# Second layer norm in place in the residual tile, eight normalises and two additions on VectorE, and last batches of three and one

## The reference

```python
# attention: favor-style, 16 heads of 16
q, k = favor(x @ Wq + bq), favor(x @ Wk + bk)   # favor: softmax over the 16 features of a head
probs = (q @ k.T) / (sum(q) + EPS)
x = layernorm(x + (probs @ (x @ Wv + bv)) @ Wo + bo)
# FFN with blockwise FP4 quantise-dequantise of every operand (blocks of 16), inner width 704
gate, up = fp4(x) @ fp4(w_gate).T, fp4(x) @ fp4(w_up).T
x = layernorm(x + fp4(silu(gate) * up) @ fp4(w_down).T)
```

## Time and profile before

| | |
|---|---|
| three runs, us | 706.77, 708.69, 709.64 (median 708.69) |
| profiled execution, us | 707.44, of which span 705.70 |
| busy share of the span | TensorE 97%, its weight loads 93%, VectorE 89%, ScalarE 82%, GpSimd 80% |
| granted TensorE clock, mean | 0.995 |
| 64 stores | 128 KB each, 1.7 us from issue to landing |

### The profile page before, as it was taken

The page is one execution under the profiler, slowest core; times in us unless marked ns, Lnnn a source line. Parts: engine busy times, 40 slices in busy tenths (PEclk is TensorE's granted clock), DMA queues, the critical chain, the costliest instruction groups (busy, mean ns, idle before and its releaser), DMA issues.

```text
span 705.7 us, 16440 instructions
## 1 busy us (share of the span) xinstructions
PE 681.2 (97%) x4782; PEld 656.9 (93%) x4782; DVE 627.4 (89%) x1498; ACT 577.1 (82%) x1355; POOL 562.0 (80%) x581
## 2 busy tenths in 40 slices
PE   6999999999999979999999999999999999999993
PEld 5999999999998869999999999999999999999983
DVE  3999988999998989999999989989899998999874
ACT  5888888887778978898877777778777898888887
POOL 3778778788877878888888898888888888888760
PEclk9999999999999999999999999999999999999999
DMA  5323322223222100000000000000000011011114
GB/s 164 94 73 86 87 76 78 83 68 91 83 79 80 39 16 1 1 2 1 1 1 2 1 2 1 2 1 1 1 1 2 25 37 47 31 46 46 51 62 142
DMA packets 40473, 30.16 MB, mean 43 GB/s; under 512 B 3776, under 2 KB 40384, under 8 KB 40384
## 3 DMA queue, kind: packets, MB, share of 16 engines
q1 hardware_dynamic: 37648, 26.88, 12.7%
q10 hardware_dynamic: 2736, 2.23, 1.1%
HBM read 20.71 MB, written 8.39 MB: 41 GB/s over the span
## 4 chain that ended last, share of the span: by engine, by line
PE 88%; ACT 4%; DVE 3%; issue 3%; DMA 1%; POOL 1%; ACTq 0%; SPq 0%; DVEq 0%; POOLq 0%
PE bank L820 66%; PE wide L938 6%; PE wide L820 5%; PE bank L853 4%; PE bank L931 2%; PE bank L851 2%; PE wide L882 2%; PE bank L921 1%; PE bank L919 1%; DMA bias_b<-L_attn_bk 1%; ACT scratch L480 1%; PE wide L865 0%; ACT dump L475 0%; ACT res L480 0%; ACT bank L449 0%
## 5 line engine op out<-in xcount | busy, mean ns | idle before, releaser
L820 PE MATMUL bank<-wf_hi,rounded 128*128 128x352 f32 (+1 forms) x1664 | 387.0, 310 | 4.0 <-DVE res L768 1.7
L820 PEld LDWEIGHTS bank<-wf_hi,rounded 128*128 128x128 f32 x1664 | 283.9, 189 | 5.2 <-issue 3.9
L820 PE MATMUL bank<-wf_lo,rounded 128*128 128x352 f32 (+1 forms) x832 | 255.2, 307 | 0.0
L820 PEld LDWEIGHTS bank<-wf_lo,rounded 128*128 128x128 f32 x832 | 157.6, 189 | 0.0
L820 PE MATMUL bank<-qkv_hi,rounded 128*128 128x512 f32 (+1 forms) x512 | 146.4, 349 | 3.1 <-ACT bank L449 3.1
L416 POOL TENSOR_TENSOR scratch<-scratch 128x704 f32<-128x704 bf16 x64 | 94.9, 1482 | 38.9 <-DVE scratch L794 38.9
L820 PEld LDWEIGHTS bank<-qkv_hi,rounded 128*128 128x128 f32 x512 | 93.0, 191 | 14.2 <-issue 3.6
L405 POOL TENSOR_TENSOR scratch<-scratch 128x704 bf16<-128x704 f32 x64 | 98.3, 1536 | 1.9 <-ACT scratch L596 1.9
L376 POOL TENSOR_TENSOR scratch<-scratch 128x512 f32<-128x512 f32 x64 | 68.0, 1063 | 39.0 <-DVE scratch L707 38.8
L411 POOL TENSOR_TENSOR scratch<-scratch 128x704 f32<-128x704 f32 x64 | 89.3, 1395 | 3.7 <-DVE scratch L765 3.7
L820 PE MATMUL bank<-qkv_lo,rounded 128*128 128x512 f32 (+1 forms) x256 | 87.1, 340 | 0.0
(11 more groups left out here) (98 smaller groups left out, 1563.7 us busy)
## 6 DMA issues: line engine op xcount, KB each, us to landing
scratch<-x_feat SPq DMA_DIRECT2D x64, 128.0 KB, 2.2
scratch<-x_tok SPq DMA_DIRECT2D x64, 128.0 KB, 2.4
out<-scratch SPq DMA_DIRECT2D x64, 128.0 KB, 1.7
scratch<-w_ffn ACTq DMA_DIRECT2D x15, 128.0 KB, 2.3
scratch<-L_attn_Wq SPq DMA_DIRECT2D x1, 256.0 KB, 3.2
scratch<-L_attn_Wk SPq DMA_DIRECT2D x1, 256.0 KB, 3.4
scratch<-L_attn_Wv SPq DMA_DIRECT2D x1, 256.0 KB, 6.0
wo<-L_attn_Wo SPq DMA_DIRECT2D x1, 256.0 KB, 4.5
```

What stands on the lines that cost most here:

```text
L820: op = pe.matmul(dst, x(c), w(c), start=first and n == 0, stop=last and n == len(terms) - 1, skip_group_check=not first)
```

## The change

The normalises of the second norm write into the residual tile itself, the four buffers `o_t` and the wait for their stores go, and the stores read from `res`. The odd tiles from 49 to 63 are normalised by VectorE (a tensor_scalar at the end of its step), the others by ScalarE as before. The batches of the second norm start at other steps: those of 8 and of 4 tiles one step earlier, and the last four tiles are a batch of three (from step 68) and a batch of one (from step 70). The addition h_c of tiles 62 and 63 moves from GpSimd to VectorE, just ahead of h_g and behind slot 0 of the next step. One more round of steps is added at the end so that all of it has its place.

```diff
--- before.py
+++ after.py
@@ -48,7 +48,9 @@
 LN_SLOTS = {1: (4,), 2: (1, 5), 3: (0, 3, 6), 4: (0, 2, 4, 6), 7: (0, 1, 2, 3, 4, 5, 6)}
 LN_A = ((0, 32, 1, 44), (32, 32, 2, 82))
 SQUARE_AT = tuple(range(9, 41)) + tuple(61 + k * 2 // 3 for k in range(32))
-LN_B = ((0, 32, 2, 38), (32, 16, 2, 54), (48, 8, 4, 62), (56, 4, 7, 66), (60, 4, 7, 70))
+LN_B = ((0, 32, 2, 38), (32, 16, 2, 54), (48, 8, 4, 61), (56, 4, 7, 65), (60, 3, 7, 68), (63, 1, 7, 70))
+LAST = 62
+BY_DVE = (49, 51, 53, 55, 57, 59, 61, 63)
 
 
 def need(eng, sem, count):
@@ -183,9 +185,6 @@
         bmx, binv = ([part(NB) for _ in range(2)] for _ in range(2))
         bs2 = [part(11 * (NB // 11 + 1)).rearrange("p (a b) -> p a b", a=11)[:, :, 0:NB // 11] for _ in range(2)]
         assert taken[0] <= until_post
-        taken[0] = until_post
-        o_t = [part(D) for _ in range(T)]
-        assert taken[0] <= until_x_in
         taken[0] = until_x_in
         hg = [part(I // 2, BF16) for _ in range(2)]
         assert taken[0] <= until_x_bo
@@ -215,18 +214,18 @@
         e_max, e_s2s, e_invs, e_xns, e_ys, e_mgs, e_cs, e_gs, x_q = (
             sem(f"e_{k}") for k in "max s2 inv xn y mg c g q".split())
         x_t, x_hi, x_lo = sem("x_t"), sem("x_hi"), sem("x_lo")
-        gu_a, gu_b, si_a, si_b, h_a, h_b, h_max, h_s2, h_inv, h_xn, h_y, h_mg, h_c, h_g, h_q = (
+        gu_a, gu_b, si_a, si_b, h_a, h_b, h_max, h_s2, h_inv, h_xn, h_y, h_mg, h_c, h_cd, h_g, h_q = (
             sem(f"b_{k}") for k in
-            "gua gub sia sib ha hb hmax hs2 hinv hxn hy hmg hc hg hq".split())
-        h_t, h_hi, h_lo, h_dup, d_s, y_s, y_sq, y_ln, y_o = (
-            sem(f"b_{k}") for k in "ht hhi hlo hdup d y ysq yln yo".split())
+            "gua gub sia sib ha hb hmax hs2 hinv hxn hy hmg hc hcd hg hq".split())
+        h_t, h_hi, h_lo, h_dup, d_s, y_s, y_sq, y_ln, y_o, y_od = (
+            sem(f"b_{k}") for k in "ht hhi hlo hdup d y ysq yln yo yod".split())
 
         block = ctx.enter_context(nc.Block())
 
 
 
         A_FROM, A_TO = -1, NS + 16
-        B_FROM, B_TO = -2, NS + 3
+        B_FROM, B_TO = -2, NS + 4
         JOIN = NT + 3
 
         def ready(m, batches):
@@ -323,8 +322,12 @@
             def stores(i):
                 for t in range(T):
                     m = T * i + t
-                    sp.wait_ge(y_o, m + 1)
-                    sp.dma_start(out[bass.ds(m * P, P), :], o_t[t]).then_inc(st_out[t], 16)
+                    by_dve = sum(n <= m for n in BY_DVE)
+                    if m in BY_DVE:
+                        sp.wait_ge(y_od, by_dve)
+                    else:
+                        sp.wait_ge(y_o, m + 1 - by_dve)
+                    sp.dma_start(out[bass.ds(m * P, P), :], res[:, rows(m)]).then_inc(st_out[t], 16)
 
             for i in range(0, NS):
                 stores(i)
@@ -399,10 +402,11 @@
                     pool.tensor_tensor(blocks(xq[:, n % T * D:(n % T + 1) * D]), blocks(e_g[e][:, half]),
                                        over(e_s2[p % 3][:, scales], XB), ALU.mult).then_inc(x_q, 1)
                 for n in tile(m - 2):
-                    need(pool, h_xn, n + 1)
-                    need(pool, h_g, n - 1)
-                    need(pool, h_mg, n + 1)
-                    pool.tensor_tensor(hc[n % 2], hxn[n % 2], hmg[n % 2], ALU.add).then_inc(h_c, 1)
+                    if n < LAST:
+                        need(pool, h_xn, n + 1)
+                        need(pool, h_g, n - 1)
+                        need(pool, h_mg, n + 1)
+                        pool.tensor_tensor(hc[n % 2], hxn[n % 2], hmg[n % 2], ALU.add).then_inc(h_c, 1)
                 for n in tile(m - 1):
                     need(pool, h_q, n - 1)
                     need(pool, h_c, n - 1)
@@ -554,8 +558,8 @@
                     act.wait_ge(a_out, NT)
                     act.wait_ge(a_qlo, NT)
                 for g, n in ready(m, LN_B):
-                    need(act, st_out[n % T], 16 * (n // T))
-                    normalise(n, o_t[n % T], y_ln, LN_OPS * (g + 1), y_o)
+                    if n not in BY_DVE:
+                        normalise(n, res[:, rows(n)], y_ln, LN_OPS * (g + 1), y_o)
                 for n in tile(m):
                     need(act, gu_a, n + 1)
                     need(act, h_a, n)
@@ -789,7 +793,14 @@
                     dve.reciprocal(e_inv[p % 2], e_s2[p % 3]).then_inc(e_invs, 1)
                 ln(0, m + 1)
                 for n in tile(m - 2):
-                    need(dve, h_c, n + 1)
+                    if n >= LAST:
+                        need(dve, h_xn, n + 1)
+                        need(dve, h_g, n - 1)
+                        need(dve, h_mg, n + 1)
+                        dve.tensor_tensor(hc[n % 2], hxn[n % 2], hmg[n % 2], ALU.add).then_inc(h_cd, 1)
+                        need(dve, h_cd, n + 1 - LAST)
+                    else:
+                        need(dve, h_c, n + 1)
                     need(dve, h_q, n - 1)
                     dve.tensor_tensor(hg[n % 2], hc[n % 2], hmg[n % 2], ALU.subtract).then_inc(h_g, 1)
                 for p in pairs(m + 3):
@@ -806,6 +817,11 @@
                     need(dve, h_s2, n - 1)
                     dve.tensor_reduce(bmx[n % 2][:, 0:NB // 2], blocks(hid[n % 2][:, 0:HALF]), axis=AX_X, op=ALU.max,
                                       apply_absolute_value=True).then_inc(h_max, 1)
+                for g, n in ready(m, LN_B):
+                    if n in BY_DVE:
+                        need(dve, y_ln, LN_OPS * (g + 1))
+                        dve.tensor_scalar(res[:, rows(n)], res[:, rows(n)], rstd[:, n:n + 1], nbias[:, n:n + 1],
+                                          ALU.mult, ALU.add).then_inc(y_od, 1)
 
             run(dve, attention, ffn)
```

## The result

The changed kernel takes 708.61 us (median of 20 runs, 706.92 to 710.22). The kernel before takes 706.90 us (20 runs, 705.73 to 710.66), so its three first runs lay high. The recorded ratio is 1.0019, with a 95% interval of 1.0011 to 1.0028: **0.8 to 2.0 us slower**, 1.3 in the middle.

The account below looks back on a forecast made before the run. TensorE was taken to bound the kernel up to 680 us, then a chain passing between engines. A later last down projection (+1.8) less the end's gain (1.17) gave +0.65 us: 708.1 profiled, 709.3 as median, range 706.4 to 712.6.

Parts of the forecast that it names:

- signs that were to mean "I am wrong": h_g(62) starting before 685.5, the granted clock falling in the tail, or TensorE waiting between 600 and 680 us.
- The stores: Normalises no longer wait for the store four tiles back: zero before 680 us and zero after it.
- The body: Steps 61 to 64: the fourth normalise and VectorE's added small operations are hidden; taken as 0, +0.5 kept for the range.
- The squares of 59: Step 64: VectorE, free at 683.0, waits until 685.38 for these squares; with h_c(62), transposes of 62 come 1.7 us late.
- the replay: The tail reckoned engine by engine in program order on the old trace's clock: last down projection 1.8 us late, +0.65 in all.
- GpSimd holding VectorE's operations: Tail: running GpSimd operations hold VectorE's SBUF operations; normalises 49 and 51 end at 692.92; without the skill's rule, 0.45 less.
- VectorE's normalise: Tail: a tensor_scalar of 128x256 in SBUF, bounded by 0.17 and 0.42 us, taken as 0.2 each.
- The end: After the last squares: 3.65 us to the last normalise, where it was 4.82, a gain of 1.17.
- The rival of the clock: Tail: TensorE idles 3.1 us and its clock falls; low for one projection, +0.2 to +0.8, 709.9; chance 0.08.
- the dearer case: Low clock lasting through the down projections of 62 and 63: +3.6, in all 712.9; chance 0.15.
- The rivals on the faster side: Tail: either the shorter tail, 706.0, chance 0.07, or the path unchanged with only the end gaining, 707.5, chance 0.10.
- The shorter tail: VectorE not kept by squares of 59, GpSimd not holding h_c(62): gains 2.5 to 3 us, 706.0; chance 0.07.

Follow-up runs that it names:

- e5: The changed kernel with six extra matmuls on TensorE between the down projection of 60 and the transposes of 62; ratio 1.0024 against the kernel before.
- e4: The kernel before, only normalising in place, storing from the residual tile and without the wait for stores; ratio 1.0007.
- e6: The changed kernel with slot 0 of the next step behind h_lo from step 64 on; ratio 1.0011 against the kernel before, tail 23.51 us.
- e9: The changed kernel with the batch of tiles 56 to 59 started at step 66 again, not 65; ratio 0.9989 against the kernel before.
- e2: The changed kernel with the additions h_c of tiles 62 and 63 back on GpSimd; ratio 1.0020 against the kernel before, tail 25.41 us.
- e10: The kernel of e2 with four extra matmuls on TensorE ahead of the transposes of 62; ratio 1.0017 against the kernel before, tail 24.03 us.
- e8: The changed kernel with slot 0 behind h_lo from step 64, later batch operations, and only h_c(63) and normalise 63 on VectorE; ratio 0.9982 against the kernel before.

## Why the prediction was right, and where its sum was off

Forecast 709.3 (range 706.4 to 712.6), slower by 0.65 us on the path; measured 708.61, and slower by 1.3 (1.25 in the tail, 0.8 to 2.0 in the times). The forecast stood on a median of three runs that lay 1.8 us above that of 20, so its level agrees partly by luck; the difference is what tests the working, and of that the sign and the way were right and the size was half. One of the signs that were to mean "I am wrong" did appear, the fallen clock; e5 shows that it isn't what made the kernel slower. The other two did not: h_g(62) started at 686.11, and TensorE waited for nothing between 600 and 680 us.

- The stores: zero, and zero in e4.
- The body: taken as 0. From TensorE's first gate product to the transposes of 61 it takes 424.67 us before (682.39 − 257.72) and 424.58 after (682.04 − 257.46). The added small operations of step 61 were hidden. The fourth normalise of step 64 was not, as foreseen: the squares of 59 were ready 0.50 later behind the transposes of 61 (2.90 instead of 2.40).
- The squares of 59: VectorE free at 682.76 and starting at 685.04, where the replay had 683.0 and 685.38 on the clock of before, 0.35 later. Shown as the cause of the late tile 62 by e6, and of the loss as a whole, with what else moves with that number, by e9. The addition h_c took 0.89, reckoned at 0.83.
- GpSimd holding VectorE's operations: the shift took 0.78 beside h_q(62). By the rule of the Trainium skill ("SBUF — State Buffer", Who interferes with whom) the normalises of 49 and 51 wait for h_q(63) if they run in the mode that takes both ports. They took 1.22 for the pair, the first of them 0.90 and over 0.15 after h_q(63), where 53 and 55, with GpSimd idle, took 0.73; the trace agrees, and the sum with that rule was the right one.
- **The term that was mis-sized most: VectorE's normalise.** I took 0.2 us, near the lower bound of 0.17, and it takes 0.41 alone, near the upper one of 0.42, with 0.32 from start to start. At the last normalise the replay is 0.66 short (22.40 instead of 21.74), in two halves.
- The first half: the addition of 61 came at 11.54 instead of 11.21, carried to the addition of 63 (17.29 instead of 16.95). Of these 0.33, 0.17 were there before the normalises: h_q(63) ended at 10.49 instead of 10.32, in the main through the additions h_c. The pair adds 0.18: the small operation behind it starts 0.39 after h_q(63) ends, reckoned at 0.21.
- The second half: from the addition of 63 to the end it took 5.11 instead of 4.79. The last normalise, with nothing behind it to hide its length, is 0.21 of the 0.32. The other two cost what was reckoned, since each takes 0.32 up to the next start but the small operation ahead of it only 0.07 or 0.08 instead of 0.2. The rest lies in the prediction's own sum: its terms, 2.60, 0.6 and 0.7, make 3.9 and not the 3.65 that it goes on with, and the small operations, a little under 0.2 each, take a part of that back. From the last squares to the end it took 3.97 (700.47 to 704.44). Added up rightly, the terms give a gain of 0.92 at the end and +0.9 in all, nearer to the 1.25 measured.
- The end: gains 0.85 (5.11 instead of 5.95) instead of 1.17.
- The rival of the clock came half true. It fell behind the predicted gap (3.05 us) and came back in time for the down projection of 62; the price given for that case was 0.2 to 0.8, and e5 found none. That the dearer case exists e2 showed in another kernel: 1.4 us.
- The rivals on the faster side didn't occur. The shorter tail was excluded for the reasons given: VectorE did wait for the squares, and with the wait gone, h_c(62) was still held by h_xn(63) (e6).

## What to carry to other kernels

In a software pipeline of in-order engines, moving the start of a side task by one step can put its first wait ahead of work on the critical path: check for each moved operation what the engine has queued behind it, and whether what it waits for is made in the same step. Here that was paid in the last steps, where TensorE no longer hides it: in the traces a single schedule number cost 2.16 us of tail, and all the rest of the change gained 0.91. Moving the start of one batch also moved other operations that are spread up to its end, so list those too. When an operation has no row, price it between bounds by its operands' size, not by the cheapest row of the same kind.

## What was not expected of the hardware

- A VectorE tensor_scalar of 128x256 in SBUF with a scale and a shift per partition takes 0.41 us (0.32 from start to start), about what the addition with a PSUM operand of the same size takes (0.42).
- The granted clock of TensorE fell behind a gap of 3.05 us (after), and in e2 at 688.8, in a gap of 1.46 us that followed one of 2.09 and 0.87 us of transposes. It did not behind 1.51 us (before), 1.76 us (e6), or the same 1.46 us with extra matmuls ahead of it (e10). In e8 it fell among gaps of up to 1.45 us that left it alone in the profiled executions of before and after. It stayed at 0.50, the lower of its two levels (1.2 GHz), for 3.4 us in the changed kernel and for over 6 us in e2, where TensorE waited again meanwhile.
- Whether a fall costs anything is a matter of what is last: nothing in the changed kernel (e5), 1.4 us in e2 (against e10).
